# Six gather stages of a graph network: edge tables stored as pairs, rows of x copied ahead, and other orders in the last stage

## The reference

```python
h = relu(layernorm(x)); x = x + L0(h)   # two rounds of: take(h @ W, src), segment_sum over dst, norms, bias
h = relu(layernorm(x)); x = x + L1(h)   # segment mean of h[src], then [h, mean] @ W.T + b
h = relu(layernorm(x)); x = x + L2(h)   # two sage_conv: h @ W_self + mean(h[src]) @ W_neigh + b
h = relu(layernorm(x))                  # L3, the edge network:
m = gelu(concat([h[src], h[dst], w]) @ We1 + be1) @ We2 + be2
u = gelu(concat([h, segment_sum(m, dst)]) @ Wu1 + bu1) @ Wu2 + bu2
x = x + layernorm(h + u) * gamma + beta
```

## Time and profile before

| | |
|---|---|
| median of 3 runs | 6177.44 us (6175.08 to 6181.75) |
| the profiled execution, its own time | 6165.11 us |
| its span in the profile | 6163.3 us |
| busy share PE / DVE / ACT / POOL | 72% / 56% / 50% / 53% |
| mean granted TensorE clock | 0.887 |
| DMA traffic | 853.63 MB, mean 139 GB/s |

### The profile page before, as it was taken

One profiled execution on the slowest core, in us unless ns is written; L12 is line 12 of the kernel. 1 busy time (PEld: TensorE's weight loads), 2 busy tenths in 40 slices (PEclk: granted clock), 3 DMA queues, 4 the chain that ended last, 5 costly groups with the idle time before them and its releaser, 6 DMA issues. The chain is left out here.

```text
span 6163.3 us, 137376 instructions
## 1 busy us (share of the span) xinstructions
PE 4459.1 (72%) x23129; PEld 3186.7 (52%) x23130; DVE 3426.8 (56%) x11286; ACT 3070.1 (50%) x6571; POOL 3247.6 (53%) x3244
## 2 busy tenths in 40 slices
PE   4556666687678886666699999877774577776776
PEld 1123333476556665555577777655653344444444
DVE  6875555453357776887333333366663455555554
ACT  7954444265456664665333333355553355555555
POOL 0015555477765676677533345354564766566660
PEclk9879999798889998987799999999997788888888
DMA  2213333133245555777444445476775455555553
GB/s 75 75 47 83 83 81 82 47 101 91 81 125 154 159 166 149 237 238 217 137 131 133 135 138 145 125 211 204 209 219 149 132 154 158 150 151 153 156 154 105
DMA packets 1039095, 853.63 MB, mean 139 GB/s; under 512 B 137464, under 2 KB 844096, under 8 KB 1039020
## 3 DMA queue, kind: packets, MB, share of 16 engines
q1 hardware_dynamic: 938668, 672.02, 35.9%
q0 software_dynamic: 100352, 180.83, 12.2%
HBM read 465.53 MB, written 386.80 MB: 138 GB/s over the span
## 5 line engine op out<-in xcount | busy, mean ns | idle before, releaser
L539 POOL DMA_INDIRECT M<-table_b,six x1176 | 1198.8, 1019 | 1076.7 <-PE banks L942 494.9
L942 PE MATMUL banks<-M,OH 128*128 x9408 | 1357.6, 305 | 308.7 <-POOLq L570 202.7
L539 POOL DMA_INDIRECT M<-table_a,six x1176 | 1233.3, 1049 | 589.1 <-issue 329.5
L942 PEld LDWEIGHTS banks<-M,OH 128*128 128x128 f32 x9408 | 1282.3, 216 | 478.5 <-issue 449.3
L1283 DVE TENSOR_TENSOR OH<-lane,dstrel 128x1024 f32<-128x1024 f32 x588 | 720.4, 1226 | 488.5 <-PE banks L942 387.8
L630 ACT ACTIVATE AG<-banks x1176 | 632.3, 589 | 699.8 <-PE banks L942 694.6
L534 POOL DMA_INDIRECT edges_by_block<-pack,pos_i x392 | 376.0, 959 | 688.5 <-DVE pos_i L1161 589.6
L933 PE MATMUL banks<-zero_h 128*128 128x512 f16 x1176 | 368.0, 395 | 392.1 <-issue 256.2
L630 ACT ACTIVATE HT<-banks 128x512 f32<-128x512 f32 x686 | 410.7, 599 | 350.6 <-PE banks L860 344.2
L860 PE MATMUL banks<-ident,HO 128*128 128x128 f32 x2352 | 379.4, 286 | 216.9 <-ACT HO L647 179.9
L539 POOL DMA_INDIRECT M<-table_dst,dix x392 | 408.6, 1042 | 119.5 <-issue 115.2
(11 more groups left out here) (267 smaller groups left out, 7992.5 us busy)
## 6 DMA issues: line engine op xcount, KB each, us to landing
XB<-state SPq DMA_DIRECT2D x392, 256.0 KB, 2.9
table_b<-T SPq DMA_DIRECT2D x784, 64.0 KB
table_a<-T SPq DMA_DIRECT2D x784, 64.0 KB
state<-T SPq DMA_DIRECT2D x196, 256.0 KB
state<-Z SPq DMA_DIRECT2D x196, 256.0 KB
h_turned<-HT SPq DMA_DIRECT2D x196, 256.0 KB
M<-messages SPq DMA_DIRECT2D x98, 512.0 KB, 4.2
XB<-in_x SPq DMA_DIRECT2D x390, 128.0 KB
```

What stands on the lines that cost most here:

```text
L539: nc.gpsimd.indirect_dma_start(out=M[:, slot, :], out_offset=None, in_=table, in_offset=bass.IndirectOffsetOnAxis(ap=idx, axis=0)).then_in ...
L942: last = mm(banks[:, ds(sums_at[k], P)], OH[:, b * US + k, :], source[:, ds(rows_at[k], P)], start=False, stop=False, skip_group_check=True)
```

## The change

Four edits:

1. Stage 1 (`placed1`): behind the four table stores of a group SyncE issues four copies of 64 KB from x to a new tensor `x_by_rank` in HBM, in rank order. Stage 2 then loads a group's rows of x with two DMAs of 128 KB from it, without the table read; there the state's store stands ahead of the table's stores, and one wait of VectorE (on ScalarE's relu) is two groups looser.
2. Stage 5 (`placed5`): `T1` and `T2` become two halves of one tile `T12`, and both go to one tensor of pairs, `table_pairs`, with four DMAs per group. Stage 6 gathers from row 2 src and row 2 dst + 1. The indices are doubled once, at the start. SyncE's parts in stage 5 stand in another order.
3. Stage 6, TensorE: the identity products of a group move from `out6` into `hidden6`, one part earlier, and two banks (5 and 7) are used in turn in place of one. `out6` no longer waits for `updated_normed`; `hidden6` waits instead for the variances of the group two before. `load6` waits for `hidden6`'s products rather than for `out6`'s.
4. Stage 6, all engines: the parts after the walk have lags one or two larger, and in the lists `load6`, `messages` and `edges6` come first.

```diff
-        q_tab = dram("table_dst", [NP, P])
+        pairs = dram("table_pairs", [2 * NP, P])
+        x_rank = dram("x_by_rank", [GROUPS, P, W4])
...
-        T1 = sb("T1", [P, 2, W4]); T2 = sb("T2", [P, 2, W4])
+        T12 = sb("T12", [P, 2, 2, W4]); T1 = T12[:, :, 0, :]; T2 = T12[:, :, 1, :]; src2T = sb("src2T", [P, TILES], I32)
...
-            staggered(sp, [(5, placed(1, tabs[1], T1, (s_t1, "t1"), st))])
+            def placed1(i, b):
+                g = 2 * i + b
+                sp.wait_ge(s_t1, g + (at(1, "t1") + 1))
+                stand(sp)
+                to = spots(g)
+                for j, r in enumerate(to):
+                    sp.dma_start(tabs[1][ds(r, P), :], q(T1[:, b, :])[:, j, :]).then_inc(st[b], 16)
+                for j, r in enumerate(to):
...
+                    sp.dma_start(q(x_rank[g])[:, j, :], a["x"][ds(r, P), :]).then_inc(sv[b], 16)
...
+            staggered(sp, [(5, placed1)])
+            kept(1, "sv", sv)
...
-                for j, r in enumerate(spots(g)):
...
-                    sp.dma_start(q(XB[:, b, :])[:, j, :], a["x"][ds(r, P), :]).then_inc(in_[b], 16)
...
+                sp.dma_start(XB[:, b, 0:2 * P], x_rank[g][:, 0:2 * P]).then_inc(in_[b], 16)
...
+                sp.dma_start(XB[:, b, 2 * P:4 * P], x_rank[g][:, 2 * P:4 * P]).then_inc(in_[b], 16)
...
+            def placed5(i, b):
+                g = 2 * i + b
+                sp.wait_ge(s_t1, g + (at(5, "t1") + 1))
+                stand(sp)
+                sp.wait_ge(s_t2, g + (at(5, "t2") + 1))
+                stand(sp)
+                for j, r in enumerate(spots(g)):
+                    sp.dma_start(pairs.rearrange("(n k) d -> n k d", k=2)[ds(r, P), :, :], T12[:, b, :, j * P:(j + 1) * P]).then_inc(st[b], 16)
...
-                need(sp, s_mm, g + (at(6, "mm") - 1))
+                need(sp, s_mma, g + (at(6, "mma") - 1))
...
-            staggered(sp, [(0, store_edges), (5, load_edges), (LEADE + 2, load6), (LEADE + 6, store6), (LEADE + 4, late6)])
+            staggered(sp, [(LEADE + 3, load6), (0, store_edges), (5, load_edges), (LEADE + 6, late6), (LEADE + 8, store6)])
...
-            staggered(act, [(LEADE + 4, hidden6), (1, messages), (LEADE + 5, deviations(6, (s_z6, 0))), (LEADE, sums(5)), (LEADE + 2, turned(6)), (LEADE + 5, normed6)])
+            staggered(act, [(1, messages), (LEADE + 5, hidden6), (LEADE, sums(5)), (LEADE + 6, deviations(6, (s_z6, 0))), (LEADE + 3, turned(6)), (LEADE + 7, normed6)])
...
+                need(pe, s_var, g + (at(6, "var") - 1))
+                for j in range(Q4):
+                    mm(q(ps[5 + 2 * b])[:, j, :], q(H[:, b, 0, :])[:, j, :], ident[:, :], start=(j == 0), stop=False, skip_group_check=True)
...
-                need(pe, s_z6, g)
...
-                    mm(o, q(H[:, b, 1, :])[:, j, :], wu2[:, :], start=True, stop=False)
-                    last = mm(o, q(H[:, b, 0, :])[:, j, :], ident[:, :], start=False, stop=True)
+                    last = mm(q(ps[5 + 2 * b])[:, j, :], q(H[:, b, 1, :])[:, j, :], wu2[:, :], start=False, stop=True, skip_group_check=True)
...
-            staggered(pe, [(0, walk(5)), (4, out6), (2, turn_rows(6, T1)), (3, hidden6)])
+            staggered(pe, [(0, walk(5)), (3, turn_rows(6, T1)), (4, hidden6), (5, out6)])
...
+                if k == 0:
+                    v.tensor_scalar(src2T[:, part], got, 2.0, None, ALU.mult)
...
-                    need(dve, s_ho, g + (at(d, "ho") - 1))
+                    need(dve, s_ho, g + (at(d, "ho") - (3 if d == 2 else 1)))
...
-            staggered(dve, [(L + 5, updated), (L - 1, onehots(5)), (L + 2, pre6), (L + 6, final), (L + 5, coefficients(6, s_z6)), (0, edges6)], chain, 6)
+            staggered(dve, [(0, edges6), (L + 6, updated), (L - 1, onehots(5)), (L + 7, coefficients(6, s_z6)), (L + 2, pre6), (L + 8, final)], chain, 6)
```

More of the change, by code:

```diff
@@ L272, in settled @@
         def settled(eng, d):
-            for what, sems in (("st", st), ("sv", sv), ("sh", sh), ("sq", sq)):
+            for what, sems in (("st", st), ("sv", sv), ("sh", sh)):
                 for k in range(2):
@@ L424, in kept @@
                     sp.wait_ge(sems[k], turns(d + 1, what))
-            staggered(sp, [(5, placed(1, tabs[1], T1, (s_t1, "t1"), st))])
+            def placed1(i, b):
[6 more added lines that the diff above has]
+                for j, r in enumerate(to):
+                    if isinstance(g, int) and g == GROUPS - 1 and j >= 2:
+                        part = slice((j - 2) * (REST // 2), (j - 1) * (REST // 2))
+                        sp.dma_start(q(x_rank[g])[part, 2, :], rest(2)[part]).then_inc(sv[b], 16)
+                        continue
+                    r = nc.s_assert_within(r, 0, (FULL - 1) * P, skip_runtime_bounds_check_because="the last two ranks are the last two blocks")
+                    sp.dma_start(q(x_rank[g])[:, j, :], a["x"][ds(r, P), :]).then_inc(sv[b], 16)
+            staggered(sp, [(5, placed1)])
+            kept(1, "sv", sv)
             def load2(i, b):
@@ L431, in load2 @@
                 stand(sp)
-                for j, r in enumerate(spots(g)):
[L433 to L437, removed]
-                    sp.dma_start(q(XB[:, b, :])[:, j, :], a["x"][ds(r, P), :]).then_inc(in_[b], 16)
-            staggered(sp, [(6, placed(2, tabs[0], T1, (s_t1, "t1"), st)), (6, whole_rows(2, states[2], T2, (s_t2, "t2"), sv)), (1, load2)])
+                sp.dma_start(XB[:, b, 0:2 * P], x_rank[g][:, 0:2 * P]).then_inc(in_[b], 16)
+                if isinstance(g, int) and g == GROUPS - 1:
+                    sp.dma_start(q(XB[:, b, :])[0:REST, 2, :], rest(2)).then_inc(in_[b], 16)
+                    return
+                sp.dma_start(XB[:, b, 2 * P:4 * P], x_rank[g][:, 2 * P:4 * P]).then_inc(in_[b], 16)
+            staggered(sp, [(6, whole_rows(2, states[2], T2, (s_t2, "t2"), sv)), (6, placed(2, tabs[0], T1, (s_t1, "t1"), st)), (1, load2)])
             kept(2, "sv", sv)
@@ L587, in chunk @@
                         for j in range(GC):
-                            gather(q_tab, dix[c // 8][:, (c % 8) * GC + j:(c % 8) * GC + j + 1], (per + c % per) * GC + j, chunk_in[per + c % per])
+                            gather(table, dix[c // 8][:, (c % 8) * GC + j:(c % 8) * GC + j + 1], (per + c % per) * GC + j, chunk_in[per + c % per])
                 whole = GROUPS // 16
@@ L1259, in _ @@
                 got = ps[n % 2][:, 0:BC]
-                v.tensor_copy((srcT, dstT, ewT)[k][:, part], got).then_inc(s_er, 1)
+                if k == 0:
+                    v.tensor_scalar(src2T[:, part], got, 2.0, None, ALU.mult)
+                if k == 1:
+                    v.tensor_scalar(dstT[:, part], got, 2.0, 1.0, ALU.mult, ALU.add).then_inc(s_er, 1)
+                else:
+                    v.tensor_copy((srcT, dstT, ewT)[k][:, part], got).then_inc(s_er, 1)
             for c in range(Q4):
@@ L1378, in updated @@
                 need(dve, s_nrm, g - 1)
-                link(v.tensor_tensor(q(Z[:, b, :]), q(ps[5]), four(bu2bc), ALU.add))
+                link(v.tensor_tensor(q(Z[:, b, :]), q(ps[5 + 2 * b]), four(bu2bc), ALU.add))
                 spread(6, b, Z[:, b, :]).then_inc(s_var, 1)
```

19 lines of the change are left out of this document (8 added, 11 removed).

## The result

| | before | after |
|---|---|---|
| median of 4 runs each, one chip | 6176.26 us (6173.42 to 6181.75) | 5853.34 us (5851.2 to 5862.42) |
| ratio, 95% interval | | 0.9482 (0.9471 to 0.9494) |
| span of the profiled execution | 6163.3 us | 5849.4 us |

What follows compares the result with a forecast made beforehand. SyncE's queue was taken to bound stage 5, VectorE stage 2, rings of waits stage 6. Terms of -202 (stage 6), -24, -93 (stage 5), -24, +5, 0, +1 took 6165 to 5828, plus 12: 5840 us, range 5770 to 5960.

Steps and rivals of the forecast that it cites:

- Both rings are cut: Stage 6: rings over `hidden6`'s load (14.16 us) and over BI go, GpSimd becomes the bound, gathers save 202 us.
- the wait for BI: Stage 6: `out6` waited 2.52 us per group for BI, taken as a second ring of nearly the same length.
- rival B: Stage 6 becomes a serial round of TensorE and VectorE, 12.9 us per group, saving 16 us, total 6026; chance 0.09.
- border: Where stage 6 begins, GpSimd's 57.97 us wait for the last table stores was to fall to 34, saving 24.
- Both signs named for the stage: Stage 5: VectorE without a wait for the state's store, and SyncE with waits of its own.
- Rival A: Transfers bound stage 5, which stays at about 662 us with the border at 58; total 5921; chance 0.13.
- the 0.59 us: Stage 2: VectorE's gap, put down to ScalarE's relu, was read as VectorE's own overhead, with VectorE setting 6.45 us.
- Rival C: Stage 2 gains as well, because the queue was its bound: 39 us less, total 5801; chance 0.11.
- at most +60: Stage 1: upper bound for the copies' cost if each issue takes 0.94 us, 6.6 us per group; 30 likelier.
- Rival D: Slower: the copies hold up stage 1; at 2 us a copy it gains 484 us, total 6319; chance 0.03.
- break-even of 1.6 us a copy: Stage 1: the issue time per copy that would eat the whole gain of 337 us, 9.3 us per group.
- the 5828 of the sum: Whole kernel: the profiled execution's 6165 us less the terms' 337, before 12 us are added for the median.

Runs made afterwards that it cites:

- the last version: The changed kernel without the copies of x, with stage 5's turned rows stored by ScalarE and `final` in 128 column pieces: 5742.96 us, ratio 0.9291.
- the two orders alone: The kernel before with, in stage 6, the load for `hidden6` first on SyncE and the messages' gelu first on ScalarE: 5917.04 us, ratio 0.9596.

## Why the prediction was right, and where it wasn't

*Stage 6* was right in size and half right in reason. GpSimd did become the bound, at 1076 us for 1078. But the prediction says "Both rings are cut", as if both had to be. The runs show one binding ring, over the load for `hidden6`; the wait for BI was a follower. Edit 3 brings nothing to the total that can be measured (0.9616 with it and the lags, 0.9596 without), and alone it costs 165 us. The end behind the gathers took 115 us in place of 127. The variances are said to come 5.0 us after the edge sums begin, "0.3 of it a wait"; the trace before has 1.02 us of wait there, so the work was 4.0. And `hidden6` did wait for them, which the prediction took for a sign of rival B: a wait is no sign that an engine binds.

*Stage 5* came out as forecast, 605 us and a border of 35.84 for 34, but by luck, for the reason was wrong. I had a pair store at 0.47 us, the queue at 4.9 us per group and VectorE as the next bound at 5.85. The store takes 2.75/4 = 0.69, which makes the 4.9 into 5.8; the last 0.3 are not accounted for. The queue still binds, at 6.08 us per group, which happens to be near VectorE's 5.85. Both signs named for the stage failed: the queue has no wait, and VectorE waits 46.1 us for the state's store. Rival A is out: the DMA share reached 0.85 with 256 GB/s, above the 0.78 of the earlier trace rows, and 0.86 with 260 in the last version, where the stage was shorter still.

*Stage 2* was right, and the reading that ScalarE doesn't make the 0.59 us too. In the changed kernel the queue has waits there (97 us in 400), the wait on ScalarE's relu is two groups looser, and the gap still stands:

```profile
2108.76 1.14 DVE L1323 SCALAR_TENSOR_TENSOR H<-AG,ndr,XB 128x128 f32 x4 [0.65 <-ACT HO L674]
```

Rival C is out, but for the 7 us that the stage got shorter.

*Stage 1* is the term that was mis-sized: +5 forecast, +57 measured with the start. Three steps were off. I took 0.47 us for the copy's issue, the price of the nearest store, where the bounds were 0.33 and 0.94; it is 0.73. The rest of the queue's work was put at 2.84 us per group and is 3.1, so a group takes the queue 6.04 us and not 4.73. And I put what can be made up while GpSimd is ahead too high: the bound of "at most +60" stands beside 2.05 us on 50 groups, which is 102, without a working for the difference. Of the 75 us that (6.04 - 4.55) us make on 50 groups, 54 stayed. Some was made up: from 1500 to 1700 us the changed kernel does 32 groups where the kernel before did 26, after 51 for 60 from 1200 to 1500. But the queue was full nearly to the stage's end, so there was no place for more. Rival D names the right mechanism, below its break-even of 1.6 us a copy.

The total is nearer than its terms. The profiled execution's 5851 us is 23 above the 5828 of the sum: 52 too much in stage 1, less 20 in stage 6 (6 of them the start of the stretch, 12 the end behind the gathers), 7 in stage 2 and 2 elsewhere. And the median lies 2 us above the profiled execution where I added 12. That these errors offset each other is luck.

## What to carry to other kernels

Cost every DMA that is added by its issue time on the queue that it goes to, and compare the queue's sum per group with the pace of the stage. Here two copies that just fitted cost 7 us, and four that didn't cost 52. A full queue alone proves nothing: look whether another engine waits for what it stores. When several waits form rings, look for the one that an order on a queue makes, cut that first, and measure before restructuring for the rest. A wait on an engine that isn't the bound costs nothing, and work moved ahead into a ring that still binds lengthens it. Work brought forward to save loads later pays only if the later stage is bound by those loads.

## What the runs showed of the hardware

The length of an indirect gather's instruction on GpSimd depends on VectorE. From the changed kernel:

```profile
5209.66 0.67 DVE L1413 TENSOR_TENSOR XB<-XB,bet 128x512 f32<-128x512 f32 x1
5209.80 1.35 POOL L564 DMA_INDIRECT M<-table_pairs,dix  x1 [0.30 <-issue]
...
5211.29 0.69 DVE L1417 TENSOR_TENSOR T<-T,XB 128x512 f32<-128x512 f32 x1
5211.45 1.34 POOL L564 DMA_INDIRECT M<-table_pairs,dix  x1 [0.30 <-issue]
```

A gather that starts while such an instruction runs ends 0.81 to 0.83 us after the instruction's end (5211.15 - 5210.33, and 5212.79 - 5211.98). One that starts just before it is not held up (5204.76 against 5204.79 us: 0.94). The border is sharp: in the gathers of stage 6 of the kernel before and of four other runs, those that start up to 0.04 us behind the start of a `tensor_tensor` with both inputs in SBUF take 0.94 us, and of those that start from 0.05 us on none ends before 0.8 us behind its end. Beside a one-hot instruction of 1.23 us a gather took up to 1.99 us in the kernel before. In the changed kernel the two engines run in step: in every chunk two of the eight gathers are hit by `final` (1.35 us) and a third by the end of a one-hot instruction (1.08). In 128 column pieces `final` costs a gather 0.09 us and less in place of 0.41, though VectorE spends 3.4 us per group on it where it spent 2.1.

The Trainium skill, "SBUF — State Buffer", section "Who interferes with whom", says that a VectorE instruction with two SBUF inputs contends with a GpSimd instruction that reads SBUF, and that the later one is blocked until the first has ended. By that rule, the trace agrees: with an input in PSUM the gather keeps its 0.94 us, also in the run of the two orders alone, where 23 gathers start more than 0.05 us behind the start of such an instruction and end within 0.7 us of its end. The same section infers that a `tensor_tensor` doesn't stall the making of descriptors; for these indirect gathers, whose indices lie in SBUF (`six`, `dix`), the 1.35 us say otherwise, and the measurement decides. That it is the reading of the indices that waits is argued from that rule, not shown.

Issue times on SyncE, per DMA: 0.48 us for a store of 64 KB, 0.73 for a copy of 64 KB from HBM to HBM, 0.69 for a pair store of 128 KB in 512-byte pieces of two tile halves, 0.35 for a load of 256 KB of whole rows. The largest has the shortest issue, so bytes don't set it; what does isn't shown.
